# A rotation in its own PSUM bank, two banks for the other jobs, and low parts and sends dealt out anew

## The chip, the cores and the metric

The kernel runs on one core of a Trainium2 chip. The metric is the device time of one execution in microseconds (us); three runs of the kernel before gave 1504.27, 1504.33 and 1508.53, median 1504.33.

## The reference, cut to what matters

Four sequences of 1024 tokens with 128 channels go through an attention block and then a mixture of experts, each with layer norms and a residual. For this change only the attention counts:

```python
q = (c_q @ w_up_q.T)...   # 16 heads of 64, from a latent of 64
k = (c_kv @ w_up_k.T)...
q, k = rope(q), rope(k)   # e*cos - o*sin, e*sin + o*cos on neighbouring channels
scores = q @ k.T / 8
out = softmax(scores) @ v
```

The experts then take each token's two best of eight (router, silu-gated hidden layer of 256), and a last layer norm and sum follow. All is float32; the kernel keeps that accuracy by splitting operands into a 16-bit high part and a 16-bit low part.

## The kernel before, in words

Attention is worked off in 32 groups: four batches times eight pairs of heads. A group g has 16 steps (two heads, two halves of the queries, four times two tiles of keys); `attend(g)` exists on every engine, and each engine walks its own written-out order. In step s TensorE makes two score tiles of 128 keys x 512 queries (lines 953 and 955), and the products of probabilities and values of step s-3 (lines 974 to 978). ScalarE exponentiates the scores (line 1245). The low part of the probabilities, the f32 value less its bf16 high half, is formed either by VectorE (line 1562) or by GpSimd (line 1993), one instruction of 128x1024 a step; `DVE_STEPS` and `LATE_DVE_STEPS` say which steps are VectorE's: six of 16, seven in the groups of `SENDING`.

Beside this, group g prepares later ones. For group g+1 it looks for each query's largest score: a matmul of q with the difference of two halves of keys ("diff"), a relu of it on ScalarE (line 1227), a matmul with the second half ("base", both line 849), and a scan on VectorE (line 1541) that adds the two and takes the maximum (`max_all`). The maxima are turned ("turn", line 853) and negated (line 1548). For group g+2 it projects q and k in four quarters ("proj", line 833) and rotates them: VectorE multiplies a quarter by cosines (line 1524) and by sines (line 1529), SP swaps neighbouring rows of the sine part by two DMAs (`swap_rows`, line 610), GpSimd subtracts (`rope_add`, line 1977), ScalarE takes the f16 high part (line 1221), GpSimd the low part over both quarters (`low_rotated`, line 1987), and VectorE the difference of the two key halves (line 1533). For group g-1 it transposes the attention output ("attn", line 866; high part on ScalarE, line 1233, low part on VectorE, line 1554) and projects it ("out", line 874; copied by ScalarE, line 1240, added by GpSimd, line 2002). In some steps of each batch there are the jobs of the neighbouring batches: layer norms, latents, residuals ("tokens", "again"; VectorE's line 1591 and 1630), router input and logits, ranks.

PSUM has eight banks: three for score tiles, two for the sums of values, and three for all these jobs. `jobs_in(g, s)` gives the jobs of a step with their place among TensorE's score and value products (0: after the first score tile, diff; 1: after the second; 2: base, after the first values; 3: after the second values). `BANK_OF` deals the banks in turn over the whole order, and `BEFORE` names for each job the one that had its bank, for whose reader TensorE waits in `free`. A rotated quarter is kept in SBUF (`rot`).

From group 14 on, GpSimd also sends the rows of tokens to their experts by indirect DMAs (line 2028): 48 sends, 24 of them in groups 14 to 29 (steps 5 and 15) and 24 in groups 30 and 31 (three steps of four). SP issues all other DMAs in one order: per group the copies of q and k for both heads (`put_both`, `put_score`, `put_lone`), the swaps, the rows of maxima.

## Time and profile before

| what | value |
|---|---|
| median of three runs | 1504.33 us |
| profiled execution, span from first to last instruction | 1526.2 us |
| TensorE matmul busy | 1417.3 us (93%) |
| VectorE busy | 1206.0 us (79%) |
| ScalarE busy | 1066.9 us (70%) |
| GpSimd busy | 1234.6 us (81%) |
| first score tile of group 0 | 57.5 us |
| first score tile of group 31 | 1286.8 us |
| first load of sorted rows for the experts | 1323.7 us |

The profiled execution has no other time of its own than its span; it is 21.9 us longer than the median of the runs. PE is TensorE, PEld its weight loads, DVE VectorE, ACT ScalarE, POOL GpSimd, SP the engine that issues DMAs. Spans of matmuls are modelled and overlap: the start of the next one tells the pace (0.22 us for 512 columns). Times in steps below are told from T, the start of the step's first score matmul.

### The profile page before, as it was taken

What the parts mean: (1) busy time and instruction counts of PE and PEld (TensorE: products, weight loads), DVE (VectorE), ACT (ScalarE), POOL (GpSimd) and SP (SyncE); (2) the same over time, 40 slices, a digit from 0 to 9 for tenths busy, and PEclk for the clock granted to TensorE, in tenths of its full rate; (3) what the DMA queues carried; (4) which work ended last, traced back from release to release, by engine and by line L of the source; (5) the groups of instructions that cost most, each with busy time, mean ns of one, the idle gap of its engine ahead of it and who ended that gap; (6) DMA issues with size and microseconds to landing.
All of it is one profiled execution on the core that took longest, in us unless ns stands there. A gap on an engine that the chain in (4) does not pass through costs nothing. (4 is left out here: it accounts for less than half of the span.)

```text
span 1526.2 us, 45381 instructions
## 1 busy us (share of the span) xinstructions
PE 1417.3 (93%) x17868; PEld 938.4 (61%) x17868; DVE 1206.0 (79%) x2687; ACT 1066.9 (70%) x2072; POOL 1234.6 (81%) x729
## 2 busy tenths in 40 slices
PE   4899999999999999998999999989999999799985
PEld 1366666666666666665666655656666565599774
DVE  7788887877788788887788789888887888865456
ACT  2777788778878777777778777767877776534334
POOL 5588998989888988996888988979889889543464
PEclk8799999999999999999999999999999999999987
DMA  5444445543233233332333233323332351143112
GB/s 170 117 112 141 139 140 143 164 129 78 71 89 85 54 78 102 81 82 64 93 82 93 74 81 95 81 65 78 79 88 64 77 175 47 47 125 91 45 53 58
DMA packets 104083, 142.34 MB, mean 93 GB/s; under 512 B 16960, under 2 KB 51520, under 8 KB 103488
## 3 DMA queue, kind: packets, MB, share of 16 engines
q1 hardware_dynamic: 100800, 133.13, 32.0%
q0 software_dynamic: 3072, 6.30, 1.4%
q8 instruction: 144, 2.36, 0.7%
q14 instruction: 67, 0.55, 0.1%
HBM read 20.49 MB, written 24.38 MB: 29 GB/s over the span
## 5 line engine op out<-in xcount | busy, mean ns | idle before, releaser
L1245 ACT ACTIVATE probs<-psum 128x512 f32<-128x512 f32 x1024 | 614.6, 603 | 200.0 <-PE psum L955 198.5
L1993 POOL TENSOR_TENSOR probs_lo<-probs 128x1024 f16<-128x1024 f32 x299 | 635.6, 2136 | 116.1 <-ACT probs L1245 114.7
L974 PE MATMUL psum<-cv,probs 128*128 128x66 f16 x4096 | 477.8, 193 | 15.2 <-POOL probs_lo L1993 8.6
L1541 DVE CUSTOM_DVE_ANT_0 scan_out<-psum,ahead 128x512 f16<-128x512 f32 x512 | 348.3, 685 | 168.4 <-PE psum L849 160.1
L976 PE MATMUL psum<-cv,probs 128*128 128x64 f16 x4096 | 477.2, 194 | 0.0
L978 PE MATMUL psum<-cv,probs_lo 128*128 128x66 f16 x4096 | 475.9, 192 | 0.0
L976 PEld LDWEIGHTS psum<-cv,probs 128*128 128x128 bf16 x4096 | 381.3, 98 | 110.7 <-issue 3.7
L974 PEld LDWEIGHTS psum<-cv,probs 128*128 128x128 bf16 x4096 | 386.1, 98 | 78.5 <-POOL probs_lo L1993 14.1
L953 PE MATMUL psum<-q_both,k_twice 128*128 128x512 f16 x1024 | 389.7, 381 | 3.1 <-ACT probs L1245 3.1
L955 PE MATMUL psum<-q_max,k_ones 65*128 65x512 f16 x1024 | 392.0, 383 | 0.0
L978 PEld LDWEIGHTS psum<-cv,probs_lo 128*128 128x128 f16 x4096 | 380.8, 98 | 0.0
L1562 DVE TENSOR_TENSOR probs_lo<-probs 128x1024 f16<-128x1024 f32 x213 | 366.6, 1721 | 1.4 <-ACT probs L1245 1.1
L1227 ACT ACTIVATE ahead<-psum 128x512 f32<-128x512 f32 x512 | 305.6, 597 | 13.7 <-PE psum L849 13.4
L849 PE MATMUL psum<-k_diff,q_lone 128*128 128x512 f16 x512 | 197.5, 386 | 18.1 <-DVE max_all L1541 10.8
L1977 POOL TENSOR_TENSOR rot<-rot,t_swapped 128x512 f32<-128x512 f32 x122 | 168.8, 1384 | 47.2 <-DMA t_swapped<-t_sin 46.9
L849 PE MATMUL psum<-qk_hi,q_lone 128*128 128x512 f16 x512 | 197.2, 385 | 9.3 <-DVE max_all L1541 5.7
L1987 POOL TENSOR_TENSOR qk_lo<-rot,qk_hi 128x1024 f16<-128x1024 f32 x62 | 160.7, 2592 | 0.0
L953 PEld LDWEIGHTS psum<-q_both,k_twice 128*128 128x128 f16 x1024 | 100.7, 98 | 88.4 <-ACT probs L1245 6.2
L955 PEld LDWEIGHTS psum<-q_max,k_ones 65*128 65x128 f16 x1024 | 99.5, 97 | 84.4 <-issue 1.6
L849 PEld LDWEIGHTS psum<-k_diff,q_lone 128*128 128x128 f16 x512 | 50.8, 99 | 91.0 <-DVE max_all L1541 24.0
L1524 DVE TENSOR_TENSOR rot<-psum,cos_sb 128x512 f32<-128x512 f32 x124 | 85.6, 691 | 11.6 <-PE psum L833 4.5
L1336 ACT ACTIVATE act_sb<-psum 128x512 f32<-128x512 f32 x63 | 37.3, 596 | 80.2 <-PE psum L1057 43.7
(224 smaller groups left out, 1927.1 us busy)
## 6 DMA issues: line engine op xcount, KB each, us to landing
t_swapped<-t_sin SPq DMA_DIRECT2D x248, 128.0 KB, 2.0
k_twice<-qk_hi SPq DMA_DIRECT2D x128, 128.0 KB
slots<-oacc SPq DMA_DIRECT2D x25, 512.0 KB, 3.1
q_lone<-qk_hi SPq DMA_DIRECT2D x64, 128.0 KB, 2.3
q_both<-qk_hi SPq DMA_DIRECT2D x64, 128.0 KB
q_both<-qk_lo SPq DMA_DIRECT2D x64, 128.0 KB
q_max<-qk_hi SPq DMA_DIRECT2D x64, 128.0 KB
k_ones<-qk_lo SPq DMA_DIRECT2D x64, 128.0 KB
```

Of the source, the lines that this page charges most:

```text
L849: pe.matmul(dst, q_lone[n % 2][a][:, t * P:(t + 1) * P], keys, start=True, stop=True).then_inc(done, 1)
L953: pe.matmul(score_ps[at], k_twice[par][h][:, k0:k0 + P], q_both[par][h][:, qh * HALF:(qh + 1) * HALF], start=True, stop=False)
L955: mm = pe.matmul(score_ps[at], k_ones[h][:, k0:k0 + P], q_max[h][:, qh * HALF:(qh + 1) * HALF], start=False, stop=True)
L974: pe.matmul(acc, high[:, q * P:(q + 1) * P, 1], v[:, 0:VLO], start=opens, stop=False, skip_group_check=True)
L976: pe.matmul(acc[:, 0:DH], high[:, q * P:(q + 1) * P, 1], v[:, VLO:VW], start=False, stop=False, skip_group_check=True)
L978: mm = pe.matmul(acc, probs_lo[t % 4][:, i, q * P:(q + 1) * P], v[:, 0:VLO], start=False, stop=kp == 3 and i == 1, skip_group_check=True)
L1227: act.activation(ahead[m % 2][:], bank[BANK_OF["diff", n, m]], ACT.Relu).then_inc(ahead_done, 1)
L1245: act.activation(probs[s % 4][:, i, :], score_ps[tile % SCORE_BANKS], ACT.Exp, scale=SCALE).then_inc(probs_done, 1)
L1541: dve.tensor_tensor_reduce(scan_out[m % 2][:], bank[BANK_OF["base", n, m]], ahead[m % 2][:], 1.0, LOWEST, ALU.add, ALU.max, max_all[a][:, ...
L1562: dve.tensor_tensor(probs_lo[s % 4][:].rearrange("p a n -> p (a n)"), p, p.bitcast(BF16).rearrange("p (n two) -> p n two", two=2)[:, :, 1] ...
L1977: pool.tensor_tensor(part, part, swap_to(n, j), ALU.subtract).then_inc(rope_sum, 1)
L1993: pool.tensor_tensor(probs_lo[s % 4][:].rearrange("p a n -> p (a n)"), p, p.bitcast(BF16).rearrange("p (n two) -> p n two", two=2)[:, :, 1 ...
```

## The change

A projected quarter of the groups from 2 on gets a bank of its own (`ROPE_BANK`, the third), and the other jobs take turns on two. The quarter stays in that bank through the whole rotation: VectorE writes the sine part to SBUF first, then multiplies by cosines in place, subtracts the swapped part in place (`rope_sum_in_bank`), ScalarE takes the high part from the bank, and VectorE the low part quarter by quarter (`low_rotated`), after which the bank is free for the next projection. GpSimd does neither the subtraction nor the low part for these groups any more. The four quarters are spread over the group: projected in steps 0, 4, 8, 12, summed in 2, 6, 10, 14, low part in 3, 7, 11, 15. The key difference is formed from the f16 high parts. VectorE forms three low parts of the probabilities (steps 4, 8, 12), GpSimd 13; the last two groups keep their split. The sends lie at steps 5 and 15 of all groups 14 to 29 and at every odd step of groups 30 and 31. SP puts the lone copies of q in two halves and has another order of swaps and copies. One job of a later batch's front moves from step 12 to 13.

```diff
-SCORE_BANKS, JOB_BANKS = 3, 3
+SCORE_BANKS, JOB_BANKS = 3, 2
+ROPE_BANK = JOB_BANKS
-PROJ_STEPS = (0, 2, 4, 6)
-ROPE_STEPS = (3, 5, 7, 9)
-HIGH_STEPS = (4, 6, 8, 10)
+PROJ_STEPS = (0, 4, 8, 12)
+SUM_STEPS = (2, 6, 10, 14)
+LOW_ROTATED_STEPS = (3, 7, 11, 15)
 DIFF_STEP = 8
-LOW_ROTATED_STEPS = (11, 13)
-DVE_STEPS = (2, 4, 6, 8, 10, 12)
-SENDING = (14, 15, 17, 18, 19, 20, 21, 22, 23, 26, 27, 28, 29)
-LATE_DVE_STEPS = {**{g: DVE_STEPS + (14,) for g in SENDING}, GROUPS - 2: ...}
+DVE_STEPS = (4, 8, 12)
+SENDING = range(14, 30)
+LATE_DVE_STEPS = {GROUPS - 2: ...}
-BANK_OF = {job: k % JOB_BANKS for k, job in enumerate(IN_ORDER)}
-BEFORE = {job: IN_ORDER[k - JOB_BANKS] if k >= JOB_BANKS else None for k, job in enumerate(IN_ORDER)}
+    banks, before, last, turn = {}, {}, {}, 0
+    for job in FRONT_JOBS + ATTENTION_JOBS:
+        if job[0] == "proj" and job[1] >= 2:
+            at = ROPE_BANK
+        else:
+            at, turn = turn % JOB_BANKS, turn + 1
+        banks[job], before[job], last[at] = at, last.get(at), job
-SEND_AT = [(g, s) for g in SENDING for s in ((15,) if g in (19, 27) else (5, 15))]
-SEND_AT += [(g, s) for g in (30, 31) for s in range(STEPS) if s % 4 < 3]
+SEND_AT = [(g, s) for g in SENDING for s in (5, 15)]
+SEND_AT += [(g, s) for g in (30, 31) for s in range(1, STEPS, 2)]
...
 (SP, order within a group)
                 put_both(g + 1, 0)
-                if g < LAST - 1:
-                    swap_rows(g + 2, 1)
                 clear_slots(g, 1)
                 put_both(g + 1, 1)
                 if g < LAST - 1:
+                    swap_rows(g + 2, 1)
+                clear_slots(g, 2)
+                if g < LAST - 1:
                     swap_rows(g + 2, 2)
-                    swap_rows(g + 2, 3)
-                clear_slots(g, 2)
                 put_score(g + 1, 0)
                 put_rows(g + 1, 0)
                 if g < LAST - 1:
-                    put_lone(g + 2)
+                    put_lone(g + 2, 0)
+                    swap_rows(g + 2, 3)
...
 (TensorE)
+                if kind == "proj" and n >= 2:
+                    pe.wait_ge(qk_lo_done, lows_rotated(n, at))
...
 (VectorE, rotate)
-                dve.tensor_tensor(rotated(n, a, t), src, cos_sb[:, cols], ALU.mult)
+                if n < 2:
+                    dve.tensor_tensor(rotated(n, j), src, cos_sb[:, cols], ALU.mult)
...
                 dve.tensor_tensor(swap_from(n, j), src, sin_sb[:, cols], ALU.mult).then_inc(proj_taken, 1)
+                if n >= 2:
+                    dve.wait_ge(proj_taken, 4 * n + (j + 1))
+                    dve.tensor_tensor(src, src, cos_sb[:, cols], ALU.mult).then_inc(cos_done, 1)
+            def rope_sum_in_bank(n, j):
+                dve.wait_ge(cos_done, 4 * (n - 2) + (j + 1))
+                dve.wait_ge(swap_in[swap_slot(n, j)], swaps_in(n, j))
+                dve.tensor_tensor(bank[ROPE_BANK], bank[ROPE_BANK], swap_to(n, j), ALU.subtract).then_inc(rope_sum, 1)
+            def low_rotated(n, j):
+                a, t = PROJ[j]
+                cols = slice(t * HALF, (t + 1) * HALF)
+                dve.wait_ge(qk_hi_done, 4 * n + (j + 1))
+                dve.tensor_tensor(qk_lo[n % 2][a][:, cols], bank[ROPE_BANK], qk_hi[n % 2][a][:, cols],
+                                  ALU.subtract).then_inc(qk_lo_done, 1)
...
 (VectorE, attend: order within a step)
+                    if g < LAST - 1 and s in SUM_STEPS:
+                        rope_sum_in_bank(g + 2, SUM_STEPS.index(s))
                     lagged(g, s, g > 0)
                     if g < LAST:
                         scan(g + 1, s)
+                    if g < LAST - 1 and s in LOW_ROTATED_STEPS:
+                        low_rotated(g + 2, LOW_ROTATED_STEPS.index(s))
...
 (GpSimd, attend)
-                    if g < LAST - 1:
-                        if s in ROPE_STEPS:
-                            rope_add(g + 2, ROPE_STEPS.index(s))
-                        for a in (1, 0):
-                            if s == LOW_ROTATED_STEPS[1 - a]:
-                                low_rotated(g + 2, a)
```

## Rows read from the trace of the kernel before

**Rows 1.** Groups 1 to 29: stretch, length, busy PE, PEld, DVE, ACT, POOL; clock, DMA.

```profile
94.00:1249.00 1155.00, 1117.05 (x14907) 712.76 (x14903) 955.64 (x2028) 890.79 (x1722) 1021.50 (x545) 1.00 0.35 96
```

**Rows 2.** Waits: who waited <- for whom: us in total, times, longest.

```profile
DVE scan_out L1541 <- PE psum L849: 160.1, 216, 3.0
...
PE psum L849 <- DVE max_all L1541: 16.5, 32, 1.5
...
PE psum L974 <- POOL probs_lo L1993: 8.6, 10, 2.5
```

**Rows 3.** Timeline of TensorE, group 9, steps 2 and 3: start us, us, what.

```profile
409.70 0.38 PE L953 MATMUL psum<-q_both,k_twice 128*128 128x512 f16 x1
...
412.16 0.38 PE L953 MATMUL psum<-q_both,k_twice 128*128 128x512 f16 x1
...
412.60 0.38 PE L849 MATMUL psum<-k_diff,q_lone 128*128 128x512 f16 x1
...
413.62 0.38 PE L849 MATMUL psum<-qk_hi,q_lone 128*128 128x512 f16 x1
414.20 0.38 PE L953 MATMUL psum<-q_both,k_twice 128*128 128x512 f16 x1
```

**Rows 4.** The same, steps 5 to 6 and 9 to 10.

```profile
416.66 0.38 PE L953 MATMUL psum<-q_both,k_twice 128*128 128x512 f16 x1
...
419.60 0.38 PE L849 MATMUL psum<-k_diff,q_lone 128*128 128x512 f16 x1
...
426.75 0.38 PE L953 MATMUL psum<-q_both,k_twice 128*128 128x512 f16 x1
...
428.31 0.38 PE L849 MATMUL psum<-qk_hi,q_lone 128*128 128x512 f16 x1
...
429.98 0.38 PE L849 MATMUL psum<-k_diff,q_lone 128*128 128x512 f16 x1
```

**Rows 5.** Timeline of ScalarE, group 9, step 3.

```profile
413.29 0.59 ACT L1227 ACTIVATE ahead<-psum 128x512 f32<-128x512 f32 x1
```

**Rows 6.** Timeline of VectorE, group 9, steps 2, 3, 8 and 9.

```profile
410.54 0.69 DVE L1554 TENSOR_TENSOR aT_lo<-psum,aT_hi 128x512 f16<-128x512 f32 x1 [0.77 <-ACT aT_hi L1233]
...
412.36 0.69 DVE L1524 TENSOR_TENSOR rot<-psum,cos_sb 128x512 f32<-128x512 f32 x1
...
413.57 1.21 DVE L1562 TENSOR_TENSOR probs_lo<-probs 128x1024 f16<-128x1024 f32 x1
414.70 0.17 DVE L1570 RECIPROCAL o_rden<-psum 128x4 f32<-128x4 f32 x1
...
427.24 0.69 DVE L1533 TENSOR_TENSOR k_diff<-rot 128x512 f16<-128x512 f32 x1
428.15 0.28 DVE L1548 TENSOR_SCALAR max_turned<-psum 8x128 f16<-8x128 f32 x1 [0.22 <-PE psum L853]
```

**Rows 7.** Timeline of VectorE and TensorE, group 16, steps 3 and 4.

```profile
689.15 5.47 DVE L1562 TENSOR_TENSOR probs_lo<-probs 128x1024 f16<-128x1024 f32 x1
...
695.70 0.08 DVE L1541 DVE_READ_ACCUMULATOR2_ANT max_all<- 128x1 f32 x1
...
695.84 0.61 PE L833 MATMUL psum<-c_both,w_hi 128*128 128x512 f16 x1 [3.87 <-DVE max_all L1541]
```

**Rows 8.** Single lines over the run: duration ns min/median/max; last, landing of the swaps.

```profile
L1562 DVE TENSOR_TENSOR probs_lo<-probs x213: 1201/1576/5475, 65.8 to 1325.8; 128x1024 f16<-128x1024 f32 x107
...
L1541 DVE CUSTOM_DVE_ANT_0 scan_out<-psum,ahead x512: 659/690/693, 39.5 to 1287.0; 128x512 f16<-128x512 f32 x171
...
L1993 POOL TENSOR_TENSOR probs_lo<-probs x299: 1882/1904/2897, 60.5 to 1328.4; 128x1024 f16<-128x1024 f32 x150
...
L1977 POOL TENSOR_TENSOR rot<-rot,t_swapped x122: 1252/1275/2544, 26.5 to 1231.9; 128x512 f32<-128x512 f32 x122
...
DMA to landing us min/median/max: 1.9/2.0/4.0
```

**Rows 9.** Timeline of VectorE, group 9, step 12: residual adds behind a scan.

```profile
437.93 1.12 DVE L1591 SCALAR_TENSOR_TENSOR res_sb<-x_sb,rstd_x,psum 128x128 f32<-128x128 f32 x4
```

More of the change, by code:

```diff
@@ L156, with place_jobs @@
 FRONT_JOBS = FRONT_PROJ[0] + FRONT_PROJ[1] + FRONT_SCANS[0] + FRONT_TURNS[:1] + FRONT_SCANS[1] + FRONT_TURNS[1:]
-IN_ORDER = FRONT_JOBS + [job for g in range(GROUPS) for s in range(STEPS) for _, job in jobs_in(g, s)]
-BANK_OF = {job: k % JOB_BANKS for k, job in enumerate(IN_ORDER)}
-BEFORE = {job: IN_ORDER[k - JOB_BANKS] if k >= JOB_BANKS else None for k, job in enumerate(IN_ORDER)}
+ATTENTION_JOBS = [job for g in range(GROUPS) for s in range(STEPS) for _, job in jobs_in(g, s)]
+def place_jobs():
+    banks, before, last, turn = {}, {}, {}, 0
[5 more added lines that the diff above has]
+        banks[job], before[job], last[at] = at, last.get(at), job
+    return banks, before
+BANK_OF, BEFORE = place_jobs()
 def dve_steps(g):
@@ L174, in low_parts_done, with lows_rotated @@
     return of is pool_steps, sum(len(of(k)) for k in range(g)) + of(g).index(step) + 1
+def lows_rotated(n, j):
+    return 2 * n if n < 2 else 4 + 4 * (n - 2) + (j + 1)
 def swap_slot(n, j):
@@ L286, in program @@
         score_ps = [psum[:, i] for i in range(SCORE_BANKS)]
-        bank = [psum[:, SCORE_BANKS + i] for i in range(JOB_BANKS)]
+        bank = [psum[:, SCORE_BANKS + i] for i in range(JOB_BANKS + 1)]
         outacc = psum[:, 6:8]
@@ L465, in swap_to, with rotated @@
             return t if swap_slot(n, j) >= 2 else t[:]
-        def rotated(n, a, t):
-            return rot_second[a][t] if n == 1 else rot[a][:, t * HALF:(t + 1) * HALF]
+        def rotated(n, j):
+            if n >= 2:
+                return bank[ROPE_BANK]
+            a, t = PROJ[j]
+            return rot_second[a][t] if n else rot[a][:, t * HALF:(t + 1) * HALF]
         def z_rows_of(n):
@@ L713, in _ @@
             put_rows(0, 0)
-            put_lone(1)
+            put_lone(1, 0)
+            put_lone(1, 1)
             put_rows(0, 1)
```

54 lines of the change are left out of this document (32 added, 22 removed).

## Prediction

> **What bounds the kernel now.** I read the busy table by stretches first, then the timeline of single steps on TensorE and VectorE, then the durations and the waits. In the attention stretch (groups 1 to 29) TensorE is busy 1117.1 of 1155 us at the full clock [rows 1]. So all idle time of TensorE there is 37.9 us, 1.3 us a group, and that is the most that any relief of the other engines can give back; VectorE (83% busy) and GpSimd (88%) have slack on average and matter only by when a result is ready. The waits say which results come late now: the matmuls of line 849 wait for VectorE's scan results (max_all) 16.5 us, those of the values for GpSimd's low parts 8.6 us [rows 2].
>
> Inside a step of group 9 everything stands at fixed distances from the step's first score matmul, T: the difference matmul (job "diff") at T+0.44, the base matmul (job "base") at T+1.46, the next step at T+2.04 when no other job is in it [rows 3]. Step 5, with attention's transposes, is 2.50 long: its successor's diff starts 2.94 after T (419.60 less 416.66). Step 9, with a turn and an output projection, is 2.79 long: diff 10 starts 3.23 after T (429.98 less 426.75), and its base, behind the turn, at 1.56 (428.31) [rows 4]. ScalarE's relu of diff ends at T+1.72 (413.29+0.59 less 412.16) [rows 5]; a scan takes VectorE 0.69 [rows 8]. TensorE starts 0.06 us after the result it waited for (695.70+0.08 to 695.84) [rows 7]. Those are the numbers for the sum.
>
> **The banks.** Today's three banks rotate over all jobs. With two, each job waits for the job two places before it. I walked the order: in a plain stretch diff waits for the diff of the step before and base for the base before; but behind each step with one extra job the roles cross, and diff of step s+1, at T+0.44, waits for the scan of step s. That happens at diff 2, 6, 8 and 10 of every group. Today diff 6 and diff 10 wait for jobs older than that (diff 5, the turn). So there the scan of step s is due 1.02 us earlier than where base s+1 alone needs it (0.44 instead of 1.46 into the next step) [rows 3].
>
> **VectorE's new order.** At steps 0, 4, 8 and 12 it forms sine part, cosine part (in the bank); the very next step begins with a low part (steps 5, 9, 13 form those of 4, 8, 12), and only then comes that step's scan. Rotation starts today 0.20 into the next step (412.36 against T=412.16), its two instructions take 1.21 together, the low part follows at once, and the next instruction 1.13 later [rows 6]. After the change the cosine part waits for the sine part to finish (two waits in place of none, 0.09 more: 0.20 to 0.88, then 0.93 to 1.62), and what follows can start at 1.54.
> - Step 5: low part 1.54 to 2.75, scan 2.67 to 3.36. Diff 6 starts at 3.42 instead of 2.94: **0.48 lost**. Queued behind that scan on VectorE is the split of attention, which base 6 waits for; TensorE is shifted by the same 0.48 then, so it adds nothing.
> - Step 9: key difference 1.54 to 2.23 (0.69 uncontended, row at 427.24; formed from f16 now, so I keep 0.28, the short instruction at 428.15, as its other end), maxima to 2.36, low part to 3.49, scan to 4.18. Diff 10 at 4.24 instead of 3.23: **1.01 lost** (0.60 at the other end) [rows 4, 6].
> - Step 13: scan ends at 3.36, base 14 needs it at 2.04+1.46=3.50: nothing lost, 0.08 to spare.
> - Steps 1 and 2: base 1 now waits for diff 1's relu (1.72+0.06=1.78, it would start at 1.56, as base 9 does): **0.22**. Base 2 waits for attention's low half, which ends 0.84+0.69=1.53 into step 2 (410.54 against T=409.70): 1.59 instead of 1.46, **0.13** [rows 3 to 6].
> The sum is 1.84 us a group; 29 groups make **+53 us** (lower end 1.43 a group, 41).
>
> **Contention.** A low part takes VectorE 1.20 at least, 1.58 in the median, 5.48 at most; scans, which read one operand from PSUM, stay within 0.66 to 0.69 [rows 8]. So only instructions with both operands in SBUF meet GpSimd. Two of the three low parts are now on TensorE's path. GpSimd has no low part of its own for steps 4, 8, 12, so it is often idle just then; it is late after its seven low parts in a row (13 to 3, 1.90 each) with a send at 15 and one at 5. Mean loss between 0 and 0.5 each; I take 0.25 each, **+15** over 29 groups (ends 0 and 29, and more in the second rival).
>
> **What goes from GpSimd:** four rotation adds (1.28 each) and two low halves (as wide as a low part, so at least 1.90) a group, 8.9 us; it gets 3 or 4 low parts more at 1.90 (5.7 to 7.6), and five groups get eight sends more between them [rows 8]. VectorE loses 3 or 4 low parts (1.58) and gets four sums and four low quarters at 0.69, uncontended, and the key difference perhaps shorter: near even. The adds and the quarters lie in steps 2, 3, 6, 7, 10, 11, 14, 15, before or after a scan that has over a microsecond to spare (0.69 added to a step that VectorE enters idle by 0.4 to 0.8). I cost them at nothing; uncovered, each late sum would cost up to 0.69. The sum waits on the swap's DMAs: sine done at 0.88 in the next step, landing 2.0 after issue [rows 8], so for the pair of DMAs at 3.0 to 3.5 into the next step, about when VectorE gets there. SP now has all eight copies of q and k ahead of swap 1, and swap 2 ahead of the score copies, which wait for half the scores anyway; a first half of the lone copies goes out early. I take nothing; the third rival is the price of a late swap. ScalarE's splits move to steps 2, 6, 10, 14, behind its second exponential, where it goes idle now; a projection waits in its own bank for the low quarter of the step before it, which VectorE ends some 3.2 into that step, over a microsecond ahead of the want: nothing for either, and past that point TensorE would wait with the whole next step behind it.
>
> What VectorE's low parts and the adds cost today goes away: the two 5.5 us low parts (groups 16 and 24) with idle TensorE behind them and its clock at 1.2 GHz afterwards (0.61 a matmul instead of 0.38) [rows 3, 7], together **-10** (the wait of 3.87 and about a microsecond at the slow clock, twice; between 0 and -14); TensorE's waits for GpSimd's low parts, **-5** of 8.6; today's waits for scans in plain groups, which the new ones swallow, **-15** of 16.5 [rows 2].
>
> **Groups beside other work.** Residual adds, second adds (two halves each, three batches): 12 jobs whose bank is freed by VectorE after four instructions of together 1.12 us behind the scan [rows 9]. The next diff now waits for them: 437.93+1.12+0.06=439.11 against a want of 437.91, 1.2 us; the second half has the rotation of step 12 ahead of it, 1.3 more. 6 of 1.2 and 6 of 2.5 are 22, today's stalls there taken off, **+15** (5 to 22). Front: its 16 scans alternate in two banks, some 0.2 each, **+3**. Tail: with half the sends in groups 30 and 31 VectorE's low parts there meet GpSimd less, **-3** (-8 to +3).
>
> Sum: 53+15-10-5-15+15+3-3 = **+53 us** on an execution of 1526.2. The three runs' median is 1504.3, 1.4% below that span; scaled, +52: **1556 us**. With both ends of the terms: 1525 to 1590.
>
> **A page's rule.** The timeline shows the contention falling only on low parts and key differences. The Trainium skill, "SBUF — State Buffer", Who interferes with whom, states just this: a VectorE instruction with at most one SBUF input does not contend with GpSimd, one with two does. The trace agrees (0.69 against up to 5.48, [rows 8]). By that rule the eight moved instructions are free of it and the first rival gains weight.
>
> **Rivals.**
> 1. Relief wins: the scans keep pace (GpSimd freed of 8.9 us a group, no long low part any more), the crossings cost little, and of the 37.9 us idle and the tail some 15 to 30 come back: about 1482. It decides if scan 5 ends by 2.88 and scan 9 by 3.17 into their steps. For it: VectorE waits 160 us for the base matmul, 216 times [rows 2], so it is early most often. Against it: that idle time lies in other steps; the chain rotation, low part, scan is already 3.1 long uncontended, and the idle to be won is bounded. 14%.
> 2. Contention decides: in the 16 sending groups the send at step 5 and the low part after it keep GpSimd going without a gap, and VectorE's low part stands behind both as at 689.15 (5.47 for 1.20) [rows 7]: half of that wait of 4.3, and the overlap, is some 2.5. 16 x 2.5 and a further 0.5 in other groups: +53 on top, 1605. 20%.
> 3. The swap is late: a landing of 4.0 (its longest) instead of 2.0 [rows 8] now stops VectorE, not GpSimd, before a scan. Were that the rule for one of four quarters, 1 us a group: 1585. 8%.
> 4. Slack hides the crossings, and nothing else moves: 1504. 5%.
> My forecast has 50%; small mixes have the rest. Within 0.3% is about 4.5 us, what a measurement of this kernel can tell from no change. Slower 0.82, same 0.05, faster 0.13. Range 1505 to 1608: the fast side and a tenth at the top stay out.
>
> **What would show it.** Diff 6 at some 3.4 and diff 10 at some 4.2 into steps 5 and 9, with the wait named as VectorE's max_all; base 1 at 1.78. Waits of TensorE for max_all going from 16.5 to 60 or more; its busy share in the stretch at 93% or less. Rotation sums and quarters at 0.69 without spread. No low part of 5 us. I am wrong if VectorE's scan 9 ends before 3.2, or if TensorE's idle time stays near 1.3 us a group.

## The result, and the profile after

The changed kernel takes 1595.83 us (median of four runs, 1589.93 to 1599.06), the kernel before on the same chip 1504.35 (four runs, 1504.27 to 1508.53): slower by 91 us, ratio 1.0596, 95% interval 1.0571 to 1.0622. The forecast was slower, 1556 us in a range of 1505 to 1608. Sign and mechanism were right, the size was short by 40 us.

The two profiled executions differ by 61.8 us only (1526.2 to 1588.0), and two things make that smaller than 91. The profile of the kernel before is 22 us above its own runs, and the profile of the changed kernel is of the fastest of its four runs (1589.93), 5.9 below their median. The first thing to settle is therefore where the profiles lie apart. The view is the busy times of a stretch, here the one from the last step of attention to the end; columns: stretch, length, busy PE, PEld, DVE, ACT, POOL (with instructions), clock, DMA share, GB/s. First the kernel before, then the changed one, then the changed one on another chip (the second experiment below).

```profile
1326.30:1526.20 199.90, 170.58 (x1542) 153.04 (x1538) 110.25 (x366) 76.18 (x162) 89.06 (x91) 0.92 0.26 75
```

```profile
1407.70:1588.00 180.30, 159.75 (x1543) 147.51 (x1540) 109.87 (x366) 76.57 (x162) 90.81 (x92) 0.95 0.30 85
```

```profile
1415.20:1617.90 202.70, 169.71 (x1542) 151.83 (x1539) 110.28 (x366) 76.58 (x162) 90.66 (x92) 0.92 0.27 75
```

Nothing in this stretch was changed, and the same kernel, the changed one, has it at 180.3 and at 202.7. So the profile of the kernel before must have come from a chip with the long form, where the kernel takes some 1527 us (first experiment below), and the first profile after from one with the short form. Attention itself starts its last step 81.4 us later (1407.7 against 1326.3); with 19.6 given back behind it that makes the 61.8. On one chip, with the stretch equal, the difference of the medians is 91, on the first chip and on another (second experiment below).

Attention's groups 1 to 29 answer to [rows 1]. 

```profile
100.10:1335.60 1235.50, 1147.71 (x14907) 713.85 (x14904) 899.46 (x2160) 900.44 (x1722) 865.27 (x479) 0.99 0.32 88
```

The stretch is 80.5 us longer for the same 14907 matmuls. TensorE's busy time grew by 30.7 (in part because behind the long stalls its matmuls take 0.61 to 0.63 instead of 0.38 each, at the 1.2 GHz level; the ends are modelled, and the rest was not taken apart), its idle time from 37.9 to 87.8. VectorE fell from 83% to 73%, GpSimd from 88% to 70%: both were relieved, as the change says, and TensorE, which sets the pace, lost. The waits answer to [rows 2]; columns: who waited for whom, us in total, times, longest.

```profile
DVE scan_out L1589 <- PE psum L878: 252.8, 307, 2.7
...
PE psum L878 <- DVE max_all L1589: 42.4, 87, 2.7
...
ACT qk_hi L1250 <- DVE psum L1565: 29.5, 32, 3.6
DVE psum L1565 <- DMA t_swapped<-t_sin: 20.9, 25, 3.6
...
PE psum L878 <- ACT ahead L1256: 16.3, 6, 2.9
...
PE psum L878 <- DVE x_sb L1678: 9.4, 6, 2.1
PE psum L878 <- DVE res_sb L1639: 9.4, 6, 2.1
...
PE psum L878 <- DVE c_later L1537: 5.5, 6, 1.2
```

The diff and base matmuls (line 878, before 849) wait for the maxima of the scans 42.4 us where they waited 16.5. Over all matmuls the rise is smaller, from 34.0 to 44.2, because in the kernel before the projections and some other jobs waited for maxima too, the projections 12.4 us, and these have their own bank now. And there are four waits which these matmuls do not show in the kernel before: for ScalarE's relu (`ahead`), for the residual and second adds (L1639, L1678) and for the latents' low half (L1537). Each of them is for a job that now stands two places ahead in the banks. VectorE's scans in turn wait for TensorE 252.8 us instead of 160.1: it has less to do and is not what sets the pace.

The crossing steps answer to [rows 3] and [rows 4]: TensorE in group 9, steps 1, 2, 5 to 6 and 9 to 10.

```profile
430.97 0.38 PE L982 MATMUL psum<-q_both,k_twice 128*128 128x512 f16 x1
...
432.74 0.39 PE L878 MATMUL psum<-qk_hi,q_lone 128*128 128x512 f16 x1
...
440.45 0.38 PE L982 MATMUL psum<-q_both,k_twice 128*128 128x512 f16 x1
...
443.87 0.39 PE L878 MATMUL psum<-k_diff,q_lone 128*128 128x512 f16 x1 [0.31 <-DVE max_all L1589]
...
450.61 0.38 PE L982 MATMUL psum<-q_both,k_twice 128*128 128x512 f16 x1
...
454.55 0.39 PE L878 MATMUL psum<-k_diff,q_lone 128*128 128x512 f16 x1 [0.33 <-DVE max_all L1589]
```

The first row of each pair is T. Base 1 starts 1.77 into its step (forecast 1.78), diff 6 starts 3.42 after T (forecast 3.42), diff 10 at 3.94 (forecast 4.24, at the other end of the key difference 3.83). VectorE in step 9 shows why the last is between; it answers to [rows 6].

```profile
450.81 0.69 DVE L1557 TENSOR_TENSOR t_sin<-psum,sin_sb 128x512 f32<-128x512 f32 x1
451.54 0.70 DVE L1560 TENSOR_TENSOR psum<-psum,cos_sb 128x512 f32<-128x512 f32 x1
452.15 0.42 DVE L1581 TENSOR_TENSOR k_diff<-qk_hi 128x512 f16<-128x512 f16 x1
452.48 0.27 DVE L1596 TENSOR_SCALAR max_turned<-psum 8x128 f16<-8x128 f32 x1
452.68 1.20 DVE L1610 TENSOR_TENSOR probs_lo<-probs 128x1024 f16<-128x1024 f32 x1
453.81 0.67 DVE L1589 CUSTOM_DVE_ANT_0 scan_out<-psum,ahead 128x512 f16<-128x512 f32 x1
```

This is the chain sine, cosine, key difference, maxima, low part, scan, without a gap; the key difference from f16 takes 0.42, where f32 took 0.69. Single lines over the run answer to [rows 8] (duration ns, min/median/max).

```profile
L1610 DVE TENSOR_TENSOR probs_lo<-probs x110: 1172/1214/3358, 75.9 to 1407.3; 128x1024 f16<-128x1024 f32 x110
...
L1581 DVE TENSOR_TENSOR k_diff<-qk_hi x30: 413/415/1002, 84.5 to 1319.1; 128x512 f16<-128x512 f16 x30
...
L1565 DVE TENSOR_TENSOR psum<-psum,t_swapped x120: 672/690/700, 70.0 to 1332.9; 128x512 f32<-128x512 f32 x120
```

The low parts have their uncontended length in the median (1214 instead of 1576 ns) and none takes 5 us. The sums in the bank hardly spread, 672 to 700.

Two kinds of long steps were not in the forecast. Group 10, steps 2 to 4: first ScalarE, then the sum on VectorE, then TensorE.

```profile
480.74 0.60 ACT L1250 ACTIVATE qk_hi<-psum 128x512 f16<-128x512 f32 x1 [0.44 <-DVE psum L1565]
481.35 1.28 ACT L1282 ACT_TABLE_LOAD   x1
482.65 0.30 ACT L1282 ACTIVATE ln_dev<-ln_mv,eps 128x8 f32<-128x8 f32 x1
482.97 1.28 ACT L1274 ACT_TABLE_LOAD   x1
484.26 0.60 ACT L1274 ACTIVATE probs<-psum 128x512 f32<-128x512 f32 x1
484.75 0.59 ACT L1256 ACTIVATE ahead<-psum 128x512 f32<-128x512 f32 x1
```

```profile
480.03 0.67 DVE L1565 TENSOR_TENSOR psum<-psum,t_swapped 128x512 f32<-128x512 f32 x1
```

```profile
485.40 0.39 PE L878 MATMUL psum<-k_diff,q_lone 128*128 128x512 f16 x1 [2.58 <-ACT ahead L1256]
```

ScalarE's copy of the high part (step 2) waits for VectorE's sum, which stands behind eight statistics; the square root of the deviations stands behind that copy and brings two table loads of 1.28 us; relu 3 is done at 485.34, and diff 4, which has diff 3's bank, starts 0.06 later. The other kind is the swap that lands late; first its two issues on SP, then the sum on VectorE, group 6, steps 2 and 3:

```profile
306.35 2.89 SPq L632 DMA_DIRECT2D t_swapped<-t_sin  x2
```

```profile
312.43 0.70 DVE L1565 TENSOR_TENSOR psum<-psum,t_swapped 128x512 f32<-128x512 f32 x1 [3.58 <-DMA t_swapped<-t_sin]
```

### The profile page after: what moved, and what is told of

Same layout as the page of the kernel before. It is cut to its first block and busy times, and to the rows that moved or that the text cites. A ratio compares the mean times of both kernels' runs of the same rounds, so it can differ in the third digit from the quotient of the medians.

```text
span 1588.0 us, 45708 instructions
## 1 busy us (share of the span) xinstructions
PE 1442.1 (91%) x17868; PEld 934.1 (59%) x17868; DVE 1139.4 (72%) x2824; ACT 1076.5 (68%) x2072; POOL 1062.5 (67%) x652
## 5 line engine op out<-in xcount | busy, mean ns | idle before, releaser
L2045 POOL TENSOR_TENSOR probs_lo<-probs 128x1024 f16<-128x1024 f32 x402 | 803.5, 2005 | 377.7 <-ACT probs L1274 376.4
L1589 DVE CUSTOM_DVE_ANT_0 scan_out<-psum,ahead 128x512 f16<-128x512 f32 x512 | 352.2, 688 | 293.2 <-PE psum L878 252.8
L878 PE MATMUL psum<-k_diff,q_lone 128*128 128x512 f16 x512 | 201.3, 393 | 73.4 <-DVE max_all L1589 22.3
L878 PE MATMUL psum<-qk_hi,q_lone 128*128 128x512 f16 x512 | 200.6, 392 | 24.0 <-DVE max_all L1589 20.1
L1610 DVE TENSOR_TENSOR probs_lo<-probs 128x1024 f16<-128x1024 f32 x110 | 145.9, 1327 | 1.3 <-ACT probs L1274 1.1
L1565 DVE TENSOR_TENSOR psum<-psum,t_swapped 128x512 f32<-128x512 f32 x120 | 82.9, 691 | 21.3 <-DMA t_swapped<-t_sin 20.9
L1557 DVE TENSOR_TENSOR t_sin<-psum,sin_sb 128x512 f32<-128x512 f32 x124 | 85.7, 691 | 11.9 <-PE psum L862 3.7
L1250 ACT ACTIVATE qk_hi<-psum 128x512 f16<-128x512 f32 x120 | 72.2, 601 | 30.2 <-DVE psum L1565 29.5
L1560 DVE TENSOR_TENSOR psum<-psum,cos_sb 128x512 f32<-128x512 f32 x120 | 83.9, 699 | 4.1
```

The lines of the kernel that those rows point to most:

```text
L878: pe.matmul(dst, q_lone[n % 2][a][:, t * P:(t + 1) * P], keys, start=True, stop=True).then_inc(done, 1)
L1557: dve.tensor_tensor(swap_from(n, j), src, sin_sb[:, cols], ALU.mult).then_inc(proj_taken, 1)
L1589: dve.tensor_tensor_reduce(scan_out[m % 2][:], bank[BANK_OF["base", n, m]], ahead[m % 2][:], 1.0, LOWEST, ALU.add, ALU.max, max_all[a][:, ...
L1610: dve.tensor_tensor(probs_lo[s % 4][:].rearrange("p a n -> p (a n)"), p, p.bitcast(BF16).rearrange("p (n two) -> p n two", two=2)[:, :, 1] ...
L2045: pool.tensor_tensor(probs_lo[s % 4][:].rearrange("p a n -> p (a n)"), p, p.bitcast(BF16).rearrange("p (n two) -> p n two", two=2)[:, :, 1 ...
```

## The experiments

Attention's length is told from the first score matmul of group 0 to that of the last step (TensorE's timeline). Each ratio is against the kernel before on the same chip, with its 95% interval. Versions of the changed kernel are compared with "changed, again" by these ratios, with 1527 us for a ratio of 1; its own interval is worth some 7 us either way, and the versions were run on different chips.

| kernel | ratio to before | attention us | last step starts |
|---|---|---|---|
| before (first profile / again) | 1 | 1268.8 / 1268.9 | 1326.3 / 1326.1 |
| changed (first profile) | 1.0596 [1.0571, 1.0622] | 1345.3 | 1407.7 |
| changed, again | 1.0605 [1.056, 1.065] | 1353.5 | 1415.2 |
| changed, low parts at 2, 6, 10 | 1.0429 [1.0383, 1.0475] | 1324.4 | 1387.2 |
| changed, three banks for jobs | 1.0137 [1.0103, 1.0170] | 1287.8 | 1344.8 |
| changed, no Sqrt tables | 1.0451 [1.0409, 1.0492] | 1324.2 | 1386.4 |
| before, dealing and sends | 1.0372 [1.0332, 1.0412] | 1325.7 | 1382.3 |
| before, sends alone | 1.0084 [1.0053, 1.0115] | 1280.0 | 1336.0 |
| before, two banks alone | 1.0574 [1.0542, 1.0606] | 1348.4 | 1410.6 |
| changed, late first sum | 1.0469 [1.0441, 1.0497] | 1338.9 | 1401.3 |
| three banks, late first sum | 0.9974 [0.9958, 0.9990] | 1257.3 | 1314.7 |
| before, groups 16, 24 and tail | 1.0078 [1.0050, 1.0106] | 1277.7 | 1334.6 |
| three banks, late sum, GpSimd roots | 0.9877 [0.9859, 0.9896] | 1247.7 | 1303.3 |

**The kernel before once more.** No edit.

> The kernel before once more, unchanged, for a second profile of it. The first one spans 1526 us where the runs take 1504. If the two low parts of 5.5 us on VectorE (groups 16 and 24) and the 200 us behind the last attention step are chance of that one execution, they are gone here: span about 1503, the stretch behind attention about 180 us. If they belong to the kernel, both are here again.

It took 1528.83 us, with a span of 1527.1. Attention is as long as before, and most groups agree within 0.6 us (group 10 is 1.7 longer, group 16 1.4 shorter); the long low parts are there again, 5.47 in group 16 and 4.25 in group 24 (5.47 before); and the stretch behind attention is again some 201 us. So neither is an accident of one execution. One row of the waits differs between the two forms of that stretch: ScalarE's `act_sb` waits for "remote" in the kernel before, and the first profile of the changed kernel has no such row.

```profile
ACT act_sb L1336 <- remote: 32.5, 7, 8.0
```

**The changed kernel once more, on another chip.** No edit.

> The changed kernel itself, on the same chip as the three beside it and, if it is the same kind as before, with the longer stretch behind attention (200 us instead of 180). Theory A (that stretch is a matter of the chip and adds to both kernels alike): ratio to the kernel before 1.05 to 1.06, its time about 1610 where the kernel before has 1527, attention's last step starts at 1407 to 1408 us again. Rival B (the changed kernel's shorter stretch is its own, since nothing of the rotation is left on GpSimd): the stretch is 180 again and the time 1590 to 1596, ratio 1.045.

Theory A: 1618.28 us against 1527.12, ratio 1.0605, the stretch behind attention 202.7 and the wait back:

```profile
ACT act_sb L1365 <- remote: 35.3, 8, 8.6
```

The long form goes with the chip and adds to both kernels alike. Attention is 8 us longer than in the first profile (1353.5 to 1345.3), more than expected: groups 16, 18, 20 and 26 are longer by 9.8 together, and why was not looked into.

**Two banks alone.** The kernel before, with all jobs but the projections on two banks and those of the third pair on in their own; rotation as before, six low parts on VectorE, sends as before.

```diff
-SCORE_BANKS, JOB_BANKS = 3, 3
+SCORE_BANKS, JOB_BANKS = 3, 2
+ROPE_BANK = JOB_BANKS
-BANK_OF = {job: k % JOB_BANKS for k, job in enumerate(IN_ORDER)}
+BANK_OF, BEFORE = place_jobs()   # as in the changed kernel
-... ("x", 1): (k, 12),
+... ("x", 1): (k, 13),
```

> The kernel before (rotation through SBUF on GpSimd, six low parts on VectorE, the sends as they were) with one part of the change alone: all jobs but the projections rotate over two banks, and the projections from the third pair on have a bank of their own. Theory A (the loss is in the two banks, whatever else VectorE does): +45 to +65 us, ratio 1.03 to 1.045; TensorE's wait for VectorE's maxima over 40 us instead of 16.5; the steps with a residual or second add and the ones behind the Sqrt tables are long as in the changed kernel. Rival B (the loss is in VectorE's new order: the rotation in the bank, low part ahead of the scan): ratio 1.00 to 1.01.

+87 us, above theory A's range: the two banks alone cost as much as the whole change (attention 1348.4 against 1345.3 and 1353.5). That the totals are so close is partly chance, for the loss lies elsewhere. Against the kernel before, step 8 of groups 1 to 29 is 18.8 longer here (in the changed kernel none of it is left once the projection that moved there is taken off), and the steps of the residual and second adds are 12 longer instead of 22. The waits and group 9's diff 6:

```profile
PE psum L861 <- DVE max_all L1553: 64.9, 118, 2.4
```

```profile
447.39 0.39 PE L861 MATMUL psum<-k_diff,q_lone 128*128 128x512 f16 x1 [1.12 <-DVE max_all L1553]
```

```profile
444.58 2.15 DVE L1574 TENSOR_TENSOR probs_lo<-probs 128x1024 f16<-128x1024 f32 x1
```

Here the low part ahead of scan 5 takes 2.15 beside GpSimd, and diff 6 comes 1.12 late: with two banks the second rival's contention is on TensorE's path, in the arrangement that still has GpSimd nearly full. Steps 4 and 5 behind the Sqrt tables are longer by 2.4 us only over the six groups, in the changed kernel by 20.1. Here no copy stands ahead of the root, and step 2 has a projection of 0.43 us in it, which gives relu 3 as much more time. The tables reach TensorE even so, group 10, step 4:

```profile
485.57 0.39 PE L861 MATMUL psum<-k_diff,q_lone 128*128 128x512 f16 x1 [1.11 <-ACT ahead L1239]
```

**Three banks for the jobs, two for the scores.** The changed kernel with the banks dealt otherwise.

```diff
-SCORE_BANKS, JOB_BANKS = 3, 2
+SCORE_BANKS, JOB_BANKS = 2, 3
-bank = [psum[:, SCORE_BANKS + i] for i in range(JOB_BANKS + 1)]
+bank = [psum[:, 3 + i] for i in range(JOB_BANKS)] + [psum[:, 2]]
```

> The changed kernel with three banks for the jobs beside the rotation's own; the bank is taken from the score tiles, which have two instead of three. Theory of the banks: all waits for the job two places before go, plain groups fall from 38.2 to about 36.7 us, residual and table-load stalls shrink: 60 to 90 us less, 1505 to 1535. ScalarE's exponentials end early enough for two score tiles (1.23 and 2.21 into a step, wanted at 2.03 and 2.7). Rival A, the moved work on VectorE and GpSimd is the cost: no gain, 1590. Rival B, score tiles now wait: slower than 1595.

Ratio 1.0137: 71 of the 91 us are gone, and a plain group (23) is at 36.7 us, from 38.2 in the changed kernel and 37.2 in the kernel before. What is left is mostly in steps 3 and 4 of ten groups, and in steps 10 and 11 of group 19 (6.1 us more than in the kernel before). With two score banks TensorE waits for exponentials, and behind those stand the waits for the sum and the swap.

```profile
ACT qk_hi L1250 <- DVE psum L1565: 50.3, 46, 3.9
...
PE psum L982 <- ACT probs L1274: 33.9, 41, 3.8
DVE psum L1565 <- DMA t_swapped<-t_sin: 29.3, 35, 3.9
```

**Low parts at steps 2, 6, 10.** They leave the steps where the rotation and the crossing fall together.

```diff
-DVE_STEPS = (4, 8, 12)
+DVE_STEPS = (2, 6, 10)
```

> The changed kernel with VectorE's three low parts at steps 2, 6, 10 (formed in 3, 7, 11) instead of 4, 8, 12 (formed behind the rotation). Theory of the crossings: diff 6 starts at 2.94 again and diff 10 near 3.4, about 1.0 us a group less, 29 groups: 30 us less than the changed kernel, about 1566. Rival, the number of low parts that GpSimd forms and contention cost the time: the numbers are the same, 1590 to 1600.

Ratio 1.0429 where the changed kernel has 1.0605, 27 us less; TensorE's wait for the maxima falls from 42.4 to 16.5. In plain groups 0.35 of step 6 goes and 0.4 to 0.5 of step 10: that is the low part ahead of the scan.

```profile
PE psum L878 <- DVE max_all L1589: 16.5, 29, 2.4
```

**No Sqrt tables.** A copy in place of both roots of the deviations; the kernel leaves out the square root there, so its layer norms in attention are not the reference's.

```diff
-act.activation(ln_dev[k][:], mv_of(k, n)[:, :, 1], ACT.Sqrt, bias=eps[:])
+act.activation(ln_dev[k][:], mv_of(k, n)[:, :, 1], ACT.Copy)
... (the same for ln_var)
```

> The changed kernel with the six standard deviations in attention taken as a copy of the variance on ScalarE (no square root, so the layer norms there are not the reference's), which takes out ScalarE's table loads in groups 10, 11, 18, 19, 26 and 27. Theory: diff 4 waits there for a relu behind two table loads, 3 to 4 us a group: 18 to 24 us less than the changed kernel, about 1574. Rival: those steps are long through other work; within 5 us of 1595.

Ratio 1.0451, 23 us less than the changed kernel; against its first profile groups 10, 11, 18, 19, 26 and 27 are shorter by 3.9, 4.1, 1.2, 6.3, 2.4 and 2.2. Steps 4 and 5 of the six are 25.4 shorter and thereby 5.3 shorter than in the kernel before: that one pays for the tables too. The forecast had no such term.

**The first sum a step later.** This asks whether the tables or the copy ahead of them cost it.

```diff
-SUM_STEPS = (2, 6, 10, 14)
-LOW_ROTATED_STEPS = (3, 7, 11, 15)
+SUM_STEPS = (3, 6, 10, 14)
+LOW_ROTATED_STEPS = (4, 7, 11, 15)   # the first at the start of step 4
```

> The changed kernel with the first rotation sum and its ScalarE split one step later (steps 3 instead of 2) and its low quarter at the start of step 4. In the changed kernel the split of step 2 stands ahead of the Sqrt of the deviations on ScalarE's queue and waits for VectorE's sum, which waits for eight statistics (or, in group 6, for the swap's DMA); the Sqrt's two table loads then make relu 3 late, and diff 4 waits for it. Theory A (that is what makes steps 3 and 4 of groups 10, 11, 18, 19, 26, 27 long, and group 6): these lose their 3 to 4 us excess each, attention is shorter by 15 to 25 us, ratio to the kernel before 1.045 to 1.05 where the changed kernel had 1.0605. Rival B (the two table loads of 1.28 us are too long for two banks wherever the split stands): less than 5 us shorter, ratio 1.057 to 1.062.

Ratio 1.0469, 21 us less, in theory A's range; the late swap of group 6 is also covered (step 3: 2.91 less, of which step 4 takes 1.44 back). ScalarE in group 10 starts the root at the start of step 3 (its first score matmul is at 476.87), without the copy ahead; below it TensorE's diff 4:

```profile
476.99 1.28 ACT L1282 ACT_TABLE_LOAD   x1
478.29 0.30 ACT L1282 ACTIVATE ln_dev<-ln_mv,eps 128x8 f32<-128x8 f32 x1
478.60 1.28 ACT L1274 ACT_TABLE_LOAD   x1
```

```profile
481.04 0.39 PE L878 MATMUL psum<-k_diff,q_lone 128*128 128x512 f16 x1 [1.54 <-ACT ahead L1256]
```

So the two loads alone still hold diff 4 up by 1.54, where copy and loads held it up by 2.58: rival B has its part. Steps 4 to 6 of the six groups give back 13.4 us against the changed kernel's second profile (11.0 against the first), where the version without tables gives back 24 to 26. Attention as a whole is 14.6 us shorter than in the second profile, a little short of the 15 expected (group 27 is 2.9 longer), and only 6.4 shorter than in the first; the 21 of the ratios carries some 8 us either way.

**The dealing alone.** The kernel before with 3 low parts for VectorE, 13 for GpSimd, and the sends of the changed kernel.

```diff
-DVE_STEPS = (2, 4, 6, 8, 10, 12)
+DVE_STEPS = (4, 8, 12)
-SENDING = (14, 15, 17, 18, 19, 20, 21, 22, 23, 26, 27, 28, 29)
+SENDING = range(14, 30)
-SEND_AT += [(g, s) for g in (30, 31) for s in range(STEPS) if s % 4 < 3]
+SEND_AT += [(g, s) for g in (30, 31) for s in range(1, STEPS, 2)]
... (SEND_AT: steps 5 and 15 in each group of SENDING; LATE_DVE_STEPS: no seventh low part)
```

> The kernel before (three banks, rotation through SBUF on GpSimd) with one part of the change alone: VectorE forms 3 low parts, GpSimd 13, and the sends spread evenly. Theory A (GpSimd is relieved by the moved rotation, and without that it can't take 13): GpSimd is 88% busy before, 35 us of 39.8 a group; 3 or 4 low parts more at 1.90 add 5.7 to 7.6 and make it 41 to 43 us a group, so it becomes the bound: +40 to +90 us over 29 groups, ratio 1.03 to 1.06, TensorE's waits for low parts above 50 us. Rival B (low parts become shorter without VectorE's beside them, as in the changed kernel, 1.83 instead of 1.90, and GpSimd keeps up): ratio 0.995 to 1.005.

The size is theory A's (+57 us), its mechanism is wrong: TensorE waits 8.1 us for GpSimd's low parts, not 50. (Rival B's 1.83 for a low part of GpSimd in the changed kernel is in no row; the medians are 1.895 there and 1.904 in the kernel before.) The loss is in step 10 of the sending groups, 4.4 to 7.0 us in eleven of them, and VectorE shows its cause, group 17:

```profile
757.20 4.98 DVE L1533 TENSOR_TENSOR k_diff<-rot 128x512 f16<-128x512 f32 x1
762.10 0.27 DVE L1548 TENSOR_SCALAR max_turned<-psum 8x128 f16<-8x128 f32 x1
```

GpSimd works without a gap from 749.36 to 761.62 here, and VectorE's key difference, 0.69 at its shortest, takes 4.98 us; the maxima behind it free the bank that diff 10 waits for. The changed kernel has the same dealing and its rotation off GpSimd, and there no key difference takes over 1.00. So the relief of GpSimd by the moved rotation is real: it is what makes this dealing bearable.

**The sends alone**, with seven low parts on VectorE in groups 14 to 29.

```diff
-SENDING = (14, 15, 17, 18, 19, 20, 21, 22, 23, 26, 27, 28, 29)
+SENDING = range(14, 30)
-... for s in ((15,) if g in (19, 27) else (5, 15))]
+... for s in (5, 15)]
-SEND_AT += [(g, s) for g in (30, 31) for s in range(STEPS) if s % 4 < 3]
+SEND_AT += [(g, s) for g in (30, 31) for s in range(1, STEPS, 2)]
```

> The kernel before with the sends spread evenly alone (two in each of groups 14 to 29, at steps 5 and 15, eight in each of 30 and 31; VectorE forms 7 low parts in all of 14 to 29). Theory A (the gain in the last two groups and in groups 16 and 24 of the changed kernel, 5 and 9 us, belongs to the dealing, not to the banks): ratio 0.990 to 0.997, groups 30 and 31 shorter by 3 to 5 us together. Rival B (a seventh low part on VectorE meets a send more often and gets 5 us long more often): ratio 1.00 to 1.01, and low parts of over 5 us in more than two groups.

Slower, 1.0084, rival B. Groups 30 and 31 do get shorter, by 6.2 us together, but steps 8 and 9 of groups 19 and 27 get longer by 8.8 and 8.6, where the send of step 5 now comes on top of those groups' normalisation on GpSimd, and group 25 by 4.2. Group 19:

```profile
825.65 8.21 DVE L1562 TENSOR_TENSOR probs_lo<-probs 128x1024 f16<-128x1024 f32 x1
```

**Groups 16 and 24, and part of the tail.**

```diff
+... 16: (4, 8, 12), 24: (4, 8, 12),   # added to LATE_DVE_STEPS
... (the two SEND_AT lines before, as above, give way to these)
+SEND_AT = [(g, s) for g in range(14, 30) if g != 25 for s in ((15,) if g in (19, 24, 27) else (5, 15))]
+SEND_AT += [(g, s) for g in (30, 31) for s in range(STEPS) if s % 2 or s in ((2, 6, 10) if g == 30 else (4, 8))]
```

> The kernel before with groups 16 and 24 dealt as in the changed kernel (VectorE forms steps 4, 8, 12) and three sends more outside the last two groups (16 at steps 5 and 15, 24 at 15), so 11 and 10 sends instead of 12 and 12 in groups 30 and 31, at steps away from the start of 31. Theory A (in groups 16 and 24 the 5.5 us low parts go with VectorE's step 2 and 6 parts, and the stall at steps 1 and 2 of group 31 is that of three sends in a row): 5 us shorter in each of groups 16 and 24 and 4 to 6 us in the last two, ratio 0.988 to 0.993. Rival B (the stall turns up at the sends' new places, as in groups 19 and 27 of the version with even sends): ratio 0.997 to 1.003.

1.0078, rival B and worse. The 5.5 us low part of group 16 is gone (steps 4 and 5: 6.7 less) and stands in group 17 instead (6.0 more), that of 24 is in its own step 6 (6.6 more) and in group 25 (steps 4 and 5, 6.4 more). Group 17:

```profile
730.25 5.80 DVE L1562 TENSOR_TENSOR probs_lo<-probs 128x1024 f16<-128x1024 f32 x1
```

With GpSimd as full as in the kernel before, redealing these groups moved that stall and didn't remove it.

**Three banks and the late first sum together.** The diffs of both, nothing else.

> The same edit on top of the version with three banks for jobs and two for scores (1.0137 before the edit): its long steps are step 3 of groups 5, 6, 10, 11, 14, 18, 19, 22, 26, 27, where VectorE's sum waits for the swap's DMA or ScalarE's split stands ahead of the tables. Theory A (both are waits for the first sum, and a step more covers them): 20 to 28 us shorter, ratio 0.995 to 1.002, no slower than the kernel before. Rival B (two score banks let ScalarE's table loads reach the score matmuls directly, whatever the split does): 0 to 8 us shorter, ratio 1.008 to 1.014.

0.9974, interval 0.9958 to 0.9990: 25 us less than without the late sum, theory A, and 0.3% below the kernel before. In the profiles groups 1 to 29 are 30.3 shorter: 10.7 in steps 3 to 5 of the six groups with tables, 12 in steps 3 and 4 of groups 5, 6, 14, 16 and 22, where no root follows, and 7 in steps 10 and 11 of groups 16, 19 and 27, for no reason that was looked for. What is left in step 3 is rival B's: two score banks let the table loads reach the score matmuls. Group 10, TensorE:

```profile
454.30 0.39 PE L982 MATMUL psum<-q_both,k_twice 128*128 128x512 f16 x1 [1.62 <-ACT probs L1274]
```

**The same, with the roots on GpSimd.**

```diff
 (ScalarE, beside attention)
-                    if (r, s) == DEV0_AT:
-                        deviations(0, n)
-                    if (r, s) == DEV1_AT:
-                        deviations(1, n)
... (GpSimd, the same two calls, and its deviations)
+pool.tensor_scalar(root_var[:], source, eps, None, ALU.add).then_inc(dev_steps, 1)
+pool.wait_ge(dev_steps, 2 * n + k + 1)
+pool.tensor_tensor(ln_dev[k][:], root_var[:], plus_half[:].to_broadcast([P, TILES]), ALU.pow).then_inc(dev_done[k], 1)
```

> The three-bank version with the late first sum (0.9974 to the kernel before), and on top of it the six square roots of the deviations formed by GpSimd (an add and a power, some 0.25 + 1.7 us as at the end of this kernel) instead of by ScalarE, whose Sqrt and the exponential behind it load a table of 1.28 us each. Theory A (with two score banks those two loads reach TensorE as 1.8 us in step 3, 0.4 to 1.2 in step 4 and a microsecond or so at the slow clock after, in each of groups 10, 11, 18, 19, 26, 27): 10 to 16 us shorter than without the edit, ratio to the kernel before 0.986 to 0.992, step 3 of those groups 2.03 again. Rival B (GpSimd's wait for VectorE's statistics delays its low part of step 2, which the values need, so that the loss only moves): ratio 0.995 to 0.999.

0.9877, interval 0.9859 to 0.9896 (1509.06 us against 1527.87): theory A. The root is an add and a power on GpSimd, and step 3 is 2.03 again in all six groups.

```profile
449.83 0.26 POOL L2129 TENSOR_SCALAR root_var<-ln_mv 128x8 f32<-128x8 f32 x1 [0.60 <-DVE ln_mv L1652]
450.18 1.67 POOL L2131 TENSOR_TENSOR ln_dev<-root_var,plus_half 128x8 f32<-128x8 f32 x1
451.82 3.75 POOL L2045 TENSOR_TENSOR probs_lo<-probs 128x1024 f16<-128x1024 f32 x2
```

Its groups 19 and 27 still have 4.6 and 3.5 us too much in step 10, with key differences of 4.75 and 4.43 us for the median 0.415:

```profile
L1579 DVE TENSOR_TENSOR k_diff<-qk_hi x30: 412/415/4754, 77.8 to 1217.7; 128x512 f16<-128x512 f16 x30
```

That is the next thing to move; it was not tried.

## Why the prediction was right, and where its sum was short

Step lengths of before and after, subtracted, give the account of the first two profiles. Groups 1 to 29: +80.5. The first row is what remains of that when the other rows of these groups are taken off.

| term | forecast | measured |
|---|---|---|
| crossings of plain steps, less today's waits (53 - 15 - 5) | +33 | +32 |
| contention on the low parts | +15 | at most +6, within other rows |
| groups 16 and 24 | -10 | -12 |
| residual and second adds | +15 | +22 |
| steps 4 and 5 behind the Sqrt tables | none | +20 |
| swap landing late (step 3), latents (step 0) | none | +5 and +3 |
| steps 14 and 15 with other batch jobs | none | +11 |
| front and group 0 | +3 | +6 |
| groups 30 and 31 | -3 | -5 |
| stretch behind attention | 0 | -20 |

**The bound and the banks: right.** That TensorE sets the pace, that diff 2, 6, 8 and 10 get the scan of the step before as their predecessor, and that steps 5 and 9 are where it costs, came out to a few hundredths of a microsecond. The sum of 1.84 a plain group is 1.54 in the trace: 0.22, 0.13 and 0.48 at base 1, base 2 and diff 6 as forecast, and 0.71 instead of 1.01 at diff 10, for the key difference took 0.42 and the larger end had been taken. (Group 23 takes 38.24, and 36.67 with three banks.) Of the 0.71 the first 0.22 are lost at base 9 already, which the forecast left out and which waits for a relu as base 1 does. Base 14 loses nothing, as forecast. Three banks give 71 us back, and two banks alone on the kernel before cost 87: with and without the rest of the change the banks are most of the loss. One sign was missed: TensorE was to wait 60 us or more for `max_all`, and its matmuls wait 44.2.

**The range: luck in part.** The measured 1595.83 lies above what the sum gave with its terms at their upper ends (1590 as written; the terms as listed give 1511 to 1593 and not 1525 to 1590). It lies in the range of 1505 to 1608 because the range reached up to the second rival, contention, and that is not what happened: contention came to 6 us at most, and terms that were not in the sum (20, 8 and 11 us in the table) filled its place.

**Contention: the wrong size, near its lower end.** The reason given against it ("GpSimd has no low part of its own for steps 4, 8, 12") fits what was measured, and the term belonged near its lower end of 0. The median low part took 1.21, and of the 87 in groups 1 to 29 four took 2.3 to 2.7, together 5.7 us above 1.20: one in step 9 of group 19, beside a key difference of 1.00 (step 10 there is 2.2 longer than in a plain group), and one in step 14 of each of groups 12, 20 and 28. The second rival did not come true here, but it did in neighbours of this change: in the kernel before and in three versions that leave GpSimd its 8.9 us a group (the dealing, the sends, groups 16 and 24) single VectorE instructions with both operands in SBUF take 5 to 8 us. In the version with two banks alone, which leaves it that work as well, none takes over 3.01, so the work alone does not decide it. The rule of the Trainium skill used in the forecast ("SBUF — State Buffer", Who interferes with whom), that a VectorE instruction with two inputs in SBUF contends with GpSimd and one with at most one does not, agrees with these rows: 4.98 for 0.69, while the sums with one operand in PSUM stay at 0.69.

**ScalarE's splits: this step failed.** The forecast said that they move behind the second exponential, "where it goes idle now", and took "nothing for either". True of plain groups. But the split of step 2 waits for a sum that waits for statistics or a swap, and ScalarE's queue behind it holds, in six groups, a root with two table loads; the prediction never listed what is queued behind the waiting instruction there. The tables and a bank order in which diff 4 waits for relu 3 are what it takes, and the split's wait makes it longer. Without the tables the excess in steps 4 to 6 of the six groups is gone, 24 to 26 us. With the split a step later about half of it is gone, 11 to 13 us, and diff 4 still waits 1.54 for relu 3 behind the two loads. With two banks and no split ahead in the kernel before the same wait is 1.11. With three banks for the jobs it moves to the score tiles (step 3 of the six groups 19.8 longer than in the kernel before), and there the roots had to leave ScalarE to end it. The whole-run figures (23 us without tables, 21 with the later sum, 25 with three banks and the later sum) contain other things too, the late swaps in the two with the later sum.

**The swap: rival 3 in part.** Its form was right, its frequency not: 25 waits of VectorE, 20.9 us in all, but only a few longer than what the slack covers (group 6, 3.58; with groups 22 and 14 some 5 us on TensorE's path). In group 6 three things add up: the sine part is done at 305.39 and the first issue starts at 306.35, behind score copies in SP's order; the two issues take 2.89 together instead of some 1.1; and the sum starts 3.19 after the end of the second, where the median landing is 2.0. In groups 14 and 22 the issues follow the sine part at once, and the landing alone is late (group 22: the sum starts 4.25 after the end of the second issue). Why a landing is late no run shows; the longest in the changed kernel is 4.8, in the kernel before 4.0.

**Residual adds and other batch jobs: mis-sized.** The gross 22 stood in the prediction's working, and "today's stalls there taken off" was not earned: 21.9 was measured. The other jobs that free a bank on VectorE (latents, router, final steps of a batch) follow the same rule and were not walked; they are most of the +14 in steps 0, 14 and 15. For the part in steps 14 and 15 the trace names several releasers, and no run separated them: this 11 us stays open.

**The 1526.2 of the profile.** The prediction scaled the sum by 1.4%. As far as the profiles show, some 20 us of the surplus of 22 lay in one unchanged stretch behind attention; no profile of the kernel before from the first chip exists to show it directly. A difference between two profiles of different chips hid 20 us of loss.

## What to carry to other kernels

When a rotation of buffers gets shorter, write down for every kind of job the new predecessor and who frees it, the rare jobs too: here the crossings in plain steps were 32 us of 81, and the rare ones made up most of the rest. A wait moved onto an in-order queue is priced by the longest thing that can stand behind it (two table loads), not by the idle time around it in a plain step. A range that holds says little by itself: here its top came from a rival that did not occur. And the change was not bad in itself: the rotation in a bank of its own frees GpSimd, and with the third job bank taken from the scores, the first sum a step later and the roots off ScalarE it is 1.2% faster than the kernel before.

## What the runs showed of the hardware that had not been expected

- VectorE formed the 512-column difference of two f16 operands in SBUF in 0.415 us (median of 30), of two f32 ones in 0.69 at the shortest (median 1.11 in the kernel before); both grow beside a GpSimd without gaps, to 4.75 (roots on GpSimd) and 8.26 (the dealing alone) at most.
- The same unchanged stretch behind attention took 180 us in one profile and 199 to 203 in the other thirteen. The one has no waits for "remote"; the others have 20 to 35 us of them on ScalarE. The profile doesn't say what these are.
- The longest low part of VectorE was 8.21 us for an uncontended 1.20, beside two low parts, two rotation adds and two normalisation steps of GpSimd in a row; a redealt group passed its stall on to its neighbour (5.47 in group 16 before, 5.80 in group 17 after).
